# A ternary feed-forward on four engines: a butterfly on GpSimd before the token rotation, three small tasks moved to ScalarE and GpSimd

## The chip, the cores and the metric

The kernel runs on one core of one Trainium2 chip. The metric is the device time of one execution in microseconds (us), the median of several runs. The engines are named as in the profile: PE is TensorE, PEld its weight loads, DVE VectorE, ACT ScalarE, POOL GpSimd, SP SyncE.

## What is computed

The reference is a network of four layers on x, four batches of 512 tokens with 512 dimensions, in float32. Each layer adds its result to x: an attention over a context (layer A), a feed-forward with ternary weights (layer B), a self-attention with 32 heads (layer C) and a routed mixture of 8 experts (layer D). The change touches layer B only:

```python
def h_bitlinear(x, w):
    xq = act_quant(fwht(x))      # 8-bit absmax quantisation per token
    wq = weight_quant(w)         # ternary, scale is mean(|w|)
    return jnp.einsum('bsh,oh->bso', xq, wq)
gate = h_bitlinear(hidden_states, w_gate)
up = h_bitlinear(hidden_states, w_up)
return h_bitlinear(jax.nn.silu(gate) * up, w_down)
```

`fwht` is the normalised Walsh-Hadamard transform along the last axis, 512 wide for the tokens and 2048 wide for the product of gate and up. The input of the layer is the normalised x (mean and deviation of each token). A Hadamard matrix of size 2n is made of four blocks H, H, H and minus H of size n, so the first half of the transform of 512 values is the 256-wide transform of the sum of their halves, and the second half that of their difference.

## The kernel before

Every engine has its own queue, in which the order of the work is written out by hand; semaphores join the queues. Layer B is done batch by batch (`phase_b(b)` on each engine, b from 0 to 3), and within a batch in tiles of 128 tokens (`st` from 0 to 3). While batch b is in its second half, the tokens of batch b+1 are made ready. The order in one batch, with the names of the functions:

- POOL: `half_rotated(b, r)` for seven of eight pairs of chunks (L848), three of the second parts of the inner rotation, `second_part_of(b, 1..3)` for their first half of 1024 columns (L853), then `normed_batch(b+2)`: after the deviation (L801) four instructions of 128x512, which subtract the mean and multiply by the reciprocal deviation (L864). `normed_batch(1)` stands at the end of layer A's part.
- PE: eight rounds of `gate_and_up` (L2580), with the transposes of the normalised tokens of batch b+1, `tokens_transposed` (L2529), within the last ones; then `tokens_rotated(b+1, st)` (L2541). This multiplies by the 512x512 Hadamard matrix, kept as four blocks of 128 rows, in two parts of the tokens each (a first part in rounded float32 and a second part, which is what the rounding left), so 8 matmuls of 512 columns for a tile. Then `inner_rotated(b, st, g)` (L2595), 8 matmuls for each of four groups g of 512 columns; between them `tokens_quantised_transposed(b+1)` (L2550), `inner_quantised_transposed(b, st)` (L2607), `down_projected(b, st)` (L2625) and `scales_spread(b+1)` (L2561). The last tiles' down projections fall between the rounds of the next batch.
- DVE: gates and their products (L1892, L1906), the last `half_rotated` (L1913), the second stage of the inner rotation (`second_stage`, L1920 and L1921, 128x1024 each), the second parts (`second_part_of`, L1926; for tile 0 both halves, for the other tiles the second half), the token scales (`token_scales`: L1834 to L1854), `inner_scales` (L1933 to L1940), quantisation (L1873, L1947); after `quantised_inner(b, 0)` it does `scale_diagonals(b+1)` (L1867, four instructions of 128x128, and L1869) and `quantised_tokens_t(b+1)` (L1885, two copies of 128x1024 bf16 from PSUM to SBUF).
- ACT: `first_part` (L1309, two of 128x1024 for a tile; the first half's semaphore releases POOL, the second's DVE), `rotated_rows` (L1316, PSUM to SBUF), `scaled_tokens` (L1287), `scaled_inner` (L1323), `inner_transposed` (L1331, one of 128x2048 bf16).

`inner_rotated(b, st, g)` waits at g = 0 for the first half's second part and at g = 2 for the second half's; `down_projected(b, 0)` waits for ACT's `inner_transposed(b, 0)`, and, because it writes the bank from which the quantised tokens are copied, for `quantised_tokens_t(b+1)`. `scales_spread` waits for the diagonals. In the fourth batch there is no next batch; in its place POOL and ACT work on the first chunks of layer C (`dims_split`, L993 and L994; `chunk_out`, L1404), and PE transposes them.

## Time and profile before

| what | us |
|---|---|
| median of 3 runs | 1669.87 |
| lowest and highest run | 1669.15, 1671.94 |
| span of the profiled execution | 1670.3 |
| layer B in the trace, roughly | 130 to 490 |
| layer C (attention), roughly | 490 to 925 |
| layer D (experts), to the end | from 925 |

The profiled execution is given by its span alone; no other time of it is recorded. Times in the trace count from the start of the span. The profile gives for each instruction when it began and how long it took; an instruction that waits inside, for a port for example, shows a longer time. The idle time of an engine stands before the instruction that ended it, with the instruction on another engine that released it. Matmuls are pipelined, so the distance of their starts, not their duration, is what one costs. Batches 1 and 2 of layer B repeat each other with a period of 89.0 us, and batch 0 ends in the same way.

### The profile page before, as it was taken

How to read it: one execution, taken by the hardware profiler on the slowest of the kernel's cores; microseconds unless marked ns; L12 is line 12 of the kernel's file. 1: busy time of each engine (PE TensorE's matmuls, PEld its weight loads, DVE VectorE, ACT ScalarE, POOL GpSimd, SP SyncE). 2: the span in 40 equal slices, each digit the busy share in tenths (PEclk: the TensorE clock that was granted, in tenths of full speed). 3: DMA queues.
4: the chain of work that ended last, by engine and by line, in shares of the span. 5: the costliest groups of instructions: out<-in, count | busy, mean ns of one | idle time of the engine just before them, and what ended most of it. 6: DMA issues, size and time to landing. Idle time of an engine off the chain costs nothing.

```text
span 1670.3 us, 24439 instructions
## 1 busy us (share of the span) xinstructions
PE 1567.2 (94%) x8124; PEld 1047.5 (63%) x8150; DVE 948.0 (57%) x1539; ACT 717.6 (43%) x1160; POOL 702.1 (42%) x479
## 2 busy tenths in 40 slices
PE   6869999999889999999899899999999999999998
PEld 4555657565543434434333778788788888788886
DVE  6998979796878897887885622222122222222221
ACT  5885646455547777777677211111111111111111
POOL 1124251633513125254354765670862180930064
PEclk9889999999898999999999999999999999999999
DMA  9189800000231445243430625231440140530088
GB/s 357 56 305 386 291 1 1 0 1 1 84 94 47 123 132 149 82 126 111 148 114 28 224 70 189 82 120 32 182 176 26 59 155 26 188 127 26 26 140 213
DMA packets 90944, 196.16 MB, mean 117 GB/s; under 512 B 7153, under 2 KB 9074, under 8 KB 90226
## 3 DMA queue, kind: packets, MB, share of 16 engines
q1 hardware_dynamic: 71746, 156.68, 28.2%
q0 software_dynamic: 7168, 17.04, 4.5%
q10 hardware_dynamic: 11952, 21.43, 3.9%
q8 instruction: 45, 0.74, 0.2%
q14 instruction: 33, 0.27, 0.1%
HBM read 113.28 MB, written 81.32 MB: 117 GB/s over the span
## 4 chain that ended last, share of the span: by engine, by line
PE 68%; DVE 16%; POOL 6%; ACT 4%; issue 3%; DMA 3%; another core or an unknown queue 0%; SPq 0%; POOLq 0%; DVEq 0%; ACTq 0%
PE psum L2929 11%; PE psum L2931 11%; PE psum L2930 11%; PE psum L2580 6%; DVE neg_max L2057 5%; PE psum L2782 5%; PE psum L2771 5%; PE psum L2744 4%; POOL expert_weight_parts L1052 3%; PE psum L2625 3%; PE psum L2595 2%; DMA w_of_even_expert<-in_L_ffn_w 2%; PE psum L2953 2%; POOL expert_weight_parts L1051 1%; DVE inner_rotated_t_second L1926 1%
## 5 line engine op out<-in xcount | busy, mean ns | idle before, releaser
L2057 DVE TENSOR_REDUCE neg_max<-psum 128x2 f32<-128x1024 f32 x248 | 291.3, 1220 | 49.5 <-PE psum L2744 48.3
L1420 ACT ACTIVATE probabilities<-psum 128x512 f32<-128x512 f32 x512 | 271.7, 601 | 85.2 <-PE psum L2771 81.3
L2199 DVE TENSOR_TENSOR expert_inner<-psum,expert_inner 128x512 f32<-128x512 f32 x78 | 53.9, 692 | 388.7 <-ACT expert_inner L1526 378.6
L2929 PE MATMUL psum<-expert_weight_parts,sorted_tokens_t_first 128*128 x624 | 250.8, 402 | 8.8 <-POOL expert_weight_parts L1052 5.1
L2930 PE MATMUL psum<-expert_weight_parts,sorted_tokens_t_first 128*128 x624 | 246.8, 396 | 0.0
L2931 PE MATMUL psum<-expert_weight_parts,sorted_tokens_t_second 128*128 x624 | 246.8, 395 | 0.0
L1526 ACT ACTIVATE expert_inner<-psum 128x512 f32<-128x512 f32 x78 | 46.7, 599 | 396.7 <-PE psum L2931 396.7
L2771 PE MATMUL psum<-query_rows,key_rows 50*128 50x512 f32 x512 | 179.3, 444 | 4.1 <-ACT probabilities L1420 3.0
L2744 PE MATMUL psum<-key_rows,query_rows 48*128 48x512 f32 x496 | 170.6, 491 | 11.7 <-DVE neg_max L2057 5.8
L2929 PEld LDWEIGHTS psum<-expert_weight_parts,sorted_tokens_t_first 128*128 128x128 f32 x624 | 117.7, 189 | 37.4 <-issue 11.1
L2782 PE MATMUL psum<-probabilities,value_and_one 128*32 128x512 f32 x1024 | 140.3, 620 | 0.8 <-ACT probabilities L1420 0.7
L2931 PEld LDWEIGHTS psum<-expert_weight_parts,sorted_tokens_t_second 128*128 128x128 f32 x624 | 117.8, 189 | 27.4
L2930 PEld LDWEIGHTS psum<-expert_weight_parts,sorted_tokens_t_first 128*128 128x128 f32 x624 | 117.9, 189 | 26.1
L2771 PEld LDWEIGHTS psum<-query_rows,key_rows 50*128 50x128 f32 x512 | 80.1, 190 | 85.2 <-ACT probabilities L1420 39.3
L1051 POOL CAST expert_weight_parts<-wo_of_expert 128x2048 fp32r<-128x2048 f32 x16 | 30.3, 1897 | 241.5 <-PE psum L2931 241.5
L1531 ACT ACTIVATE expert_inner_t_first<-psum 128x512 fp32r<-128x512 f32 x78 | 42.5, 596 | 201.8 <-PE psum L2953 201.8
L2929 PE MATMUL psum<-expert_weight_parts,expert_inner_t_first 128*128 128x512 f32 x312 | 125.8, 403 | 1.6 <-DVE expert_inner_t_second L2209 1.6
L2931 PE MATMUL psum<-expert_weight_parts,expert_inner_t_second 128*128 128x512 f32 x312 | 122.3, 392 | 0.0
L2930 PE MATMUL psum<-expert_weight_parts,expert_inner_t_first 128*128 128x512 f32 x312 | 121.9, 391 | 0.0
L2226 DVE TENSOR_SCALAR expert_out<-psum,row_weight 128x512 f32<-128x512 f32 x39 | 29.3, 751 | 160.8 <-PE psum L2931 156.8
L1010 POOL TENSOR_TENSOR x_tiles<-x_tiles,attended_normed 128x256 f32<-128x256 f32 x31 | 22.7, 733 | 211.2 <-DVE attended_normed L2104 211.2
L2595 PE MATMUL psum<-hadamard,inner_rotated_t_first 128*128 128x512 f32 x256 | 104.5, 408 | 7.0 <-DVE inner_rotated_t_second L1926 7.0
(316 smaller groups left out, 2924.3 us busy)
## 6 DMA issues: line engine op xcount, KB each, us to landing
sorted_x<-zero_rows SPq DMA_DIRECT2D x9, 3960.0 KB, 30.5
w_of_odd_expert<-in_L_ffn_w SPq DMA_DIRECT2D x8, 2048.0 KB
wo_of_expert<-in_L_ffn_wo SPq DMA_DIRECT2D x7, 2048.0 KB, 8.6
query_rows<-query_rows_of_units SPq DMA_DIRECT2D x64, 192.0 KB, 3.5
w_of_even_expert<-in_L_ffn_w SPq DMA_DIRECT2D x6, 2048.0 KB, 11.6
sorted_tokens<-sorted_x ACTq DMA_DIRECT2D x39, 264.0 KB, 2.8
sorted_y<-expert_out ACTq DMA_DIRECT2D x39, 256.0 KB
query_rows_of_units<-dims_first SPq DMA_DIRECT2D x32, 256.0 KB
```

What stands on the lines that cost most here:

```text
L1052: last = nc.gpsimd.tensor_tensor(w_r[:, at + BLOCK + s:at + BLOCK + s + BLOCK // 2], w, first_part, ALU.subtract)
L1420: nc.scalar.activation(prob[t % 2][:, i * SEQ:(i + 1) * SEQ], bank[4 + n % 3], ACT.Exp, scale=HD ** -0.5).then_inc(c_e, 1)
L2057: nc.vector.tensor_reduce(of_pair[:, p, st, :], ring(("max", (m, i))).rearrange("p (h n) -> p h n", h=2), AX.X, ALU.max, negate=True).then ...
L2199: nc.vector.tensor_tensor(h, bank[2 * half + 1], h, ALU.mult).then_inc(e_h, 1)
L2580: last = nc.tensor.matmul(bank[4 + 2 * w + h], wgu_t[w][:, k * FF + f * P:k * FF + (f + 1) * P], q_t[:, k * SEQ:(k + 1) * SEQ], start=(k = ...
L2595: last = nc.tensor.matmul(bank[4 + g], y[:, at:at + P], had[:, k * D:(k + 1) * D], start=(k + part == 0), stop=(k + part == DC))
L2744: done = nc.tensor.matmul(ring(job)[:, h * SEQ:(h + 1) * SEQ], q_r[m % 4][rows, p * SEQ + st * P:p * SEQ + (st + 1) * P], k_r[m % 4][rows, ...
L2771: nc.tensor.matmul(bank[4 + n % 3], k_r[u % 4][rows, t * P:(t + 1) * P], q_r[u % 4][rows, p * SEQ:(p + 1) * SEQ], start=True, stop=True).t ...
L2782: last = nc.tensor.matmul(bank[7][32 * h:32 * h + 32, :], v_u[u % KVH][:, t * 32:(t + 1) * 32], prob[t % 2][:, h * SEQ:(h + 1) * SEQ], sta ...
L2929: nc.tensor.matmul(out_bank, hi[:, cols], w_r[:, bass.ds(w_at, 512)], start=start, stop=False)
L2930: nc.tensor.matmul(out_bank, hi[:, cols], w_r[:, bass.ds(w_at + BLOCK, 512)], start=False, stop=False)
L2931: return nc.tensor.matmul(out_bank, lo[:, cols], w_r[:, bass.ds(w_at, 512)], start=False, stop=stop)
```

## The change

The four edits in words:

1. `normed_batch` on POOL makes, for each tile, the sum and the difference of the two halves of x (two instructions of 128x256), then normalises each half in place (the sum with twice the mean, the difference without a mean): 16 instructions and a small one for twice the mean, where there were four. `tokens_rotated(b, st)` for b of 1 to 3 multiplies with 256 columns of the first two blocks of the Hadamard matrix: 8 matmuls of 256 columns for a tile.
2. The second part of tile 0's second half goes from DVE to POOL, where it stands before the other second parts.
3. The scale diagonals of batches 1 to 3 go from DVE to ACT, after `inner_transposed(b, 0)`.
4. The two copies of the transposed quantised tokens of batches 1 to 3 go from DVE to ACT, after `first_part(b, 3)` and before `rotated_rows(b, 2, 0)`.

The diff, cut to its core (batch 0's tokens keep the old way):

```diff
def second_part(b, st, h):
 
-            if st and h == 0:
-                return b_zlo, (ST - 1) * b + st
-            return b_zlo0, (ST + 1) * b + st + h + 1
+            if h != (st == 0):
+                return b_zlo0, ST * b + st + 1
+            return b_zlo, ST * b + st + 1
...
             def second_part_of(b, st):
-                pool.wait_ge(b_zhi, 2 * (b * ST + st) + 1)
-                half = HALVES[0]
+                h = int(st == 0)
+                pool.wait_ge(b_zhi, 2 * (b * ST + st) + h + 1)
+                half = HALVES[h]
...
+                c.inc(nc.gpsimd.tensor_tensor(twice_mean[:], mv[:, 0:2 * ST:2], mv[:, 0:2 * ST:2], ALU.add))
+                halves = [[h_n[:, st * D + h * D // 2:st * D + (h + 1) * D // 2] for h in range(2)] for st in range(ST)]
                 for st in range(ST):
-                    nc.gpsimd.tensor_scalar(h_n[:, st * D:(st + 1) * D], tiles(X, b * ST + st), mv[:, 2 * st:2 * st + 1],
-                                            rstd[:, st:st + 1], ALU.subtract, ALU.mult).then_inc(b_normed, 1)
+                    x = [X[:, (b * ST + st) * D + h * D // 2:(b * ST + st) * D + (h + 1) * D // 2] for h in range(2)]
+                    c.inc(nc.gpsimd.tensor_tensor(halves[st][0], x[0], x[1], ALU.add))
+                    c.inc(nc.gpsimd.tensor_tensor(halves[st][1], x[0], x[1], ALU.subtract))
+                c.wait()
+                for st in range(ST):
+                    c.inc(nc.gpsimd.tensor_scalar(halves[st][0], halves[st][0], twice_mean[:, st:st + 1],
+                                                  rstd[:, st:st + 1], ALU.subtract, ALU.mult))
+                    nc.gpsimd.tensor_scalar(halves[st][1], halves[st][1], rstd[:, st:st + 1], None, ALU.mult).then_inc(b_normed, 1)
...
+                second_part_of(b, 0)
                 for st in range(1, ST):
                     second_part_of(b, st)
...
             def scaled_token(b, st):
-                act.wait_ge(b_fac, b + 1)
+                act.wait_ge(b_fac, 2 * b + 1)
...
+            def scale_diagonals(b):
+                act.wait_ge(b_fac, 2 * (b + 1))
+                for st in range(ST):
+                    last = nc.scalar.activation(diag[:, st * P:(st + 1) * P], ident[:], ACT.Copy, scale=tok_scale[:, st:st + 1])
+                last.then_inc(b_dg, 1)
+
+            def quantised_tokens_t(b):
+                for half in range(2):
+                    act.wait_ge(b_qt, b * ST + 2 * half + 2)
+                    nc.scalar.activation(q_t[:].rearrange("p (k t n) -> p t k n", k=DC, t=ST)[:, 2 * half:2 * half + 2],
+                                         bank_b[2 + half].rearrange("p (t k n) -> p t k n", t=2, k=DC), ACT.Copy).then_inc(b_qts, 1)
...
                 first_part(b, 3)
+                if more:
+                    quantised_tokens_t(b + 1)
                 rotated_rows(b, 2, 0)
...
                 inner_transposed(b, 0)
+                if more:
+                    scale_diagonals(b + 1)
                 scaled_inner(b, 1)
...
             def token_scale_columns(b):
                 for st in range(ST):
                     s = slice(st, st + 1)
-                    c.inc(nc.vector.tensor_scalar(tok_scale[:, s], am_c[:, s], 1.0 / 127.0, None, ALU.mult))
+                    last = nc.vector.tensor_scalar(tok_scale[:, s], am_c[:, s], 1.0 / 127.0, None, ALU.mult)
+                last.then_inc(b_fac, 1)
...
-            def scale_diagonals(b):
-                c.wait()
-                if b == 0:
-                    dve.wait_ge(a_sim, BATCH * ST)
+            def first_scale_diagonals():
+                dve.wait_ge(b_fac, 2)
+                dve.wait_ge(a_sim, BATCH * ST)
                 for st in range(ST):
                     last = nc.vector.tensor_scalar(diag[:, st * P:(st + 1) * P], ident[:], tok_scale[:, st:st + 1], None, ALU.mult)
                 last.then_inc(b_dg, 1)
+
+            def inner_scale_made(b):
+                dve.wait_ge(b_fac, 2 * (b + 1))
                 c.inc(nc.vector.tensor_scalar(inner_scale[b % 2][:], tok_scale[:], w_mean[:, 1:2], HAD_FF, ALU.mult, ALU.mult))
...
                 second_part_of(b, 0, 0)
-                second_part_of(b, 0, 1)
                 second_stage(b, 1)
...
                 if more:
-                    scale_diagonals(b + 1)
-                    quantised_tokens_t(b + 1)
+                    inner_scale_made(b + 1)
                 second_part_of(b, 3, 1)
...
                     for part, h in enumerate((first_part_at(b)[:, st * D + k * P:st * D + (k + 1) * P], h_lo(b, st)[:, k * P:(k + 1) * P])):
-                        last = nc.tensor.matmul(bank[st], h, had[:, k * D:(k + 1) * D], start=(k + part == 0), stop=(k + part == DC))
+                        if b == 0:
+                            last = nc.tensor.matmul(bank[st], h, had[:, k * D:(k + 1) * D], start=(k + part == 0), stop=(k + part == DC))
+                        else:
+                            half, j = k // 2, k % 2
+                            last = nc.tensor.matmul(bank[st][:, half * D // 2:(half + 1) * D // 2], h, had[:, j * D:j * D + D // 2],
+                                                    start=(j + part == 0), stop=(j + part == 2))
```

## Rows read from the trace of the kernel before

**Rows 1.** The page's first part: busy time of each engine over the span.
```profile
PE 1567.2 (94%) x8124; PEld 1047.5 (63%) x8150; DVE 948.0 (57%) x1539; ACT 717.6 (43%) x1160; POOL 702.1 (42%) x479
```

**Rows 2.** Busy time by stretches of one batch; columns as in the header.
```profile
core 0: us, PE busy (x) PEld busy (x) DVE busy (x) ACT busy (x) POOL busy (x), PEclk, DMA share, GB/s
...
249.20:338.20 89.00, 85.79 (x452) 55.25 (x457) 76.59 (x138) 48.03 (x57) 36.04 (x22) 1.00 0.00 1
...
427.20:516.20 89.00, 72.64 (x353) 44.63 (x355) 73.81 (x91) 44.18 (x54) 25.42 (x35) 0.85 0.30 83
```

**Rows 3.** Waits of PE within 249.2 to 338.2 us: total, times, longest us.
```profile
PE psum L2550 <- DVE uantised_tokens_of_batch L1873: 1.5, 1, 1.5
PE psum L2625 <- DVE quantised_t L1885: 1.0, 1, 1.0
PE psum L2625 <- ACT inner_quantised_t L1331: 0.3, 1, 0.3
```

**Rows 4.** Chain that ended last, at 282.7 us: start us, us, what.
```profile
282.73 3.40 PE psum L2625 x15
```

**Rows 5.** DVE timeline, 249 to 258 us: start, us, engine, line, op, tiles, idle.
```profile
252.05 0.69 DVE L1829 TENSOR_TENSOR ormed_tiles_t_second<-psum,normed_tiles_t_first 128x512 fp32r<-128x512 f32 x1 [0.23 <-ACT normed_tiles_t_first L1283]
...
256.13 2.36 DVE L1926 TENSOR_TENSOR inner_rotated_t_second<-inner_t,inner_rotated_t_first 128x1024 fp32r<-128x1024 f32 x2 [0.53 <-ACT inner_rotated_t_first L1309]
```

**Rows 6.** DVE timeline, 269 to 284 us.
```profile
271.10 2.27 DVE L1926 TENSOR_TENSOR inner_rotated_t_second<-inner_t,inner_rotated_t_first 128x1024 fp32r<-128x1024 f32 x1
...
276.90 1.21 DVE L1947 TENSOR_SCALAR quantised_tokens<-normed_or_scaled_tokens 128x2048 bf16<-128x2048 f32 x1
278.04 3.00 DVE L1867 TENSOR_SCALAR token_scale_diagonals<-ident,token_scale 128x128 f32<-128x128 f32 x4
...
281.09 1.27 DVE L1885 COPY quantised_t<-psum 128x1024 bf16<-128x1024 bf16 x2
```

**Rows 7.** POOL timeline, 255 to 296 us.
```profile
269.88 2.40 POOL L853 TENSOR_TENSOR inner_rotated_t_second<-inner_t,inner_rotated_t_first 128x1024 fp32r<-128x1024 f32 x1 [5.55 <-ACT inner_rotated_t_first L1309]
278.15 2.41 POOL L853 TENSOR_TENSOR inner_rotated_t_second<-inner_t,inner_rotated_t_first 128x1024 fp32r<-128x1024 f32 x1 [5.86 <-ACT inner_rotated_t_first L1309]
```

**Rows 8.** ACT timeline, 264 to 300 us.
```profile
277.01 2.01 ACT L1309 ACTIVATE inner_rotated_t_first<-inner_t 128x1024 fp32r<-128x1024 f32 x2 [2.25 <-DVE inner_t L1921]
278.93 1.07 ACT L1316 ACTIVATE inner_rotated_rows<-psum 128x512 f32<-128x512 f32 x2
279.88 1.88 ACT L1331 ACTIVATE inner_quantised_t<-psum 128x2048 bf16<-128x2048 bf16 x1
```

**Rows 9.** ACT groups by line and form: xcount, busy us, mean ns, idle.
```profile
L1165 ACT ACTIVATE down_ternary_t<-psum 128x1024 bf16<-128x1024 bf16 x6 | 6.0, 1004 | 0.0
...
L1113 ACT ACTIVATE kv_gram<-psum 128x128 f32<-128x128 f32 x4 | 1.1, 269 | 1.9 <-PE psum L2346 1.9
```

**Rows 10.** POOL groups by line and form, same columns.
```profile
L864 POOL TENSOR_SCALAR normed_tokens_of_batch<-x_tiles,ln_mean_var,ln_rstd 128x512 f32<-128x512 f32 x12 | 28.2, 2358 | 0.3
...
L1010 POOL TENSOR_TENSOR x_tiles<-x_tiles,attended_normed 128x256 f32<-128x256 f32 x31 | 22.7, 733 | 211.2 <-DVE attended_normed L2104 211.2
```

**Rows 11.** PE timeline, 247 to 258 us.
```profile
249.17 0.39 PE L2541 MATMUL psum<-hadamard,ormed_tiles_t_second 128*128 128x512 f32 x1
...
250.56 0.39 PE L2541 MATMUL psum<-hadamard,ormed_tiles_t_second 128*128 128x512 f32 x1
250.79 1.03 PE L2529 MATMUL psum<-ident,normed_tokens_of_batch 128*128 128x128 f32 x8
```

**Rows 12.** PE timeline, 428 to 436 us, fourth batch.
```profile
434.97 0.76 PE L2595 MATMUL psum<-hadamard,inner_rotated_t_first 128*128 128x512 f32 x1 [7.04 <-DVE inner_rotated_t_second L1926]
435.53 0.63 PE L2595 MATMUL psum<-hadamard,inner_rotated_t_second 128*128 128x512 f32 x1
```

**Rows 13.** Busy time in the attention stage, columns as rows 2.
```profile
624.80:628.20 3.40, 2.37 (x17) 1.02 (x17) 3.01 (x5) 2.10 (x4) 3.40 (x3) 1.00 0.04 8
628.20:631.60 3.40, 3.40 (x18) 1.78 (x10) 2.23 (x5) 1.27 (x4) 3.40 (x3) 0.50 0.36 92
```

More of the change, by code:

```diff
@@ L112, in network @@
         rstd = keep.tile("ln_rstd", [P, ST])
+        twice_mean = keep.tile("ln_twice_mean", [P, ST])
         half_neg = keep.tile("minus_half", [P, ST])
@@ L1812, in phase_a @@
                 token_scale_columns(0)
-                scale_diagonals(0)
+                first_scale_diagonals()
+                inner_scale_made(0)
                 sum_reciprocals(3)
@@ L1823, in phase_a @@
                 weight_out(17)
-                quantised_tokens_t(0)
+                first_quantised_tokens_t()
                 weight_out(19)
@@ L1878, in quantised_tokens, with first_quantised_tokens_t @@
                     quantised_token(b, st)
-            def quantised_tokens_t(b):
-                if b == 0:
-                    dve.wait_ge(a_done, BATCH * ST)
+            def first_quantised_tokens_t():
+                dve.wait_ge(a_done, BATCH * ST)
                 for half in range(2):
-                    dve.wait_ge(b_qt, b * ST + 2 * half + 2)
+                    dve.wait_ge(b_qt, 2 * half + 2)
                     nc.vector.tensor_copy(q_t[:].rearrange("p (k t n) -> p t k n", k=DC, t=ST)[:, 2 * half:2 * half + 2],
```

## The prediction

> **What bounds the kernel now.** I read the page's busy times first: PE is busy for 94% of the span [rows 1], but that is an average over four layers. The busy time by batch is the second view. In batch 1 of layer B PE is busy for 85.79 of 89.00 us and DVE for 76.59, ACT for 48.03 and POOL for 36.04, all at full clock (1.00); in the fourth batch the clock's mean is 0.85 [rows 2]. So PE has 3.2 us of idle time in a batch, and only this, or work that PE drops while nobody else is late, can be won. The third view says who ends that idle time: DVE's quantised tokens 1.5 us, DVE's copy `quantised_t` before the down projection 1.0, ACT's `inner_quantised_t` 0.3, DVE's second part of the tokens 0.2 [rows 3]. In the chain of waits the down projection of tile 0 starts at 282.73 [rows 4]. The question for every edit is thus which wait ends last at 250 to 258 us, at 273 and at 282.7; the same times plus 89.0 hold for batch 2, less 89.0 for batch 0.
>
> **The butterfly on PE.** Matmuls of 512 columns start 0.232 us apart (seven starts from 249.17 to 250.56) [rows 11], so a tile costs 1.86 us and the 12 tiles of batches 1 to 3 cost 22 us. No row has 256 columns of this type. The nearest rows bound one: below, half of 0.232; above, the same 0.232, if the weight load sets the pace. The eight transposes of 128 columns begin at 250.79 and the next matmul at 251.58 [rows 11], about 0.10 each, so a weight load fits into 0.12, and I take half: 0.93 us off a tile, 3.7 off a batch, 11.1 in all. The Trainium skill (TensorE: Matmul & The Clock Gate, "Back-to-back issue gap") gives 262 cycles for 256 columns and 518 for 512; by it 0.85 us would leave each tile.
>
> This is what the tile costs, not what the time gains. The next work on PE, `inner_rotated(1, 0, 0)`, needs DVE's second part, which begins at 256.13 after 0.53 us of waiting for ACT [rows 5] and takes 1.2; PE's last rotation matmul starts at about 257.4. Both arrive together: PE's work is hidden under the DVE chain from the last gates through half rotation, second stage and ACT's first part. Only one link of that chain waits for PE: DVE waited 0.23 us at 252.05 for ACT's first part of the tokens [rows 5]. So the halving brings 0.2 to 0.3 us a batch at this point, and PE is idle for the other 3.4 us in several pieces. The ends for the sum are 0 and 11.1 us; I take 0, since the next meeting point (273.3, below) doesn't move.
>
> **The second part to POOL.** DVE loses half of 2.36 us [rows 5], 1.18. POOL takes 2.40 for one [rows 7]. The two engines don't run such work side by side: DVE's L1926 at 271.10 took 2.27 us instead of 1.18 while POOL's ran from 269.88 to 272.28; 272.28 and 1.1 is its end, 273.37 [rows 6, 7]. The four diagonals at 278.04 took 3.00 us beside POOL's at 278.15 for the same reason. The new POOL instruction becomes ready at about 256.9, just when DVE goes on with the second stage of tile 1, two instructions with both inputs in SBUF. So DVE waits for 2.40 and saves 1.18 and 0.3: its token scales come 0.9 us later, not 1.2 earlier. This is covered: 0.9 us later, DVE would come to L1926 at 272.0, and POOL holds it until 272.28 in any case [rows 6, 7]. I take 0; with that cover gone it costs 0.9 a batch. The rule against this edit is in the Trainium skill (GPSIMD Engine Reference, "Engine selection" and "Key points"): elementwise work on two tensors belongs on VectorE, and GpSimd shares its SBUF interfaces with VectorE. The trace agrees, 2.40 against 1.18.
>
> **Diagonals and copies to ACT.** DVE loses 3.05 us (278.04 to 281.09) less 0.2 for the inner scale, and 1.2 for the copies [rows 6]. Its next instruction, L1926 of tile 3, meets POOL's, which ends at 280.56 [rows 7], and so ends near 281.7, not 283.4. That relieves `inner_scales(1)`, for which PE doesn't wait [rows 3].
> ACT gets the work on the path. After `first_part` (277.01, 2.01 us) it now goes on at 278.93 with the rows and at 279.88 with `inner_quantised_t`, 1.88 [rows 8]. The new copies stand before these. A copy of 1024 bf16 columns from PSUM costs 1.00 on ACT [rows 9], two cost 1.9 with their overlap of 0.1. So `inner_quantised_t` starts at 281.8, ends at 283.7, and PE begins 0.25 later, at 283.9 instead of 282.73 [rows 4]: 1.2 us late. The ends for the copies: below, DVE's 0.64 each [rows 6], which gives 0.5 us a batch; above, the 2.01 of `first_part` for two, 1.3. From there PE is never idle for long [rows 3], so all of it stays: three batches, **+3.6 us**. The queue behind the copies: `rotated_rows(2, 0)`, whose bank PE wants only after the down projection, and `scaled_inner(1)`, which is earlier anyway. The four diagonals cost at most 0.27 each [rows 9], 1.1 us, done by 284.8; `scales_spread` comes after the down projection: 0.
>
> **POOL's normalisation.** Before: four of 2.08 (mean with collisions 2.36) [rows 9, 10], 8.3 to 9.4 us. After: eight of 0.733 [rows 10] are 5.9, four two-step ones of 1.04 (half of 2.08) and four one-step ones of 0.5 to 1.04, in all 12 to 14.5. The 3 to 6 us more lie in POOL's 53 idle us a batch [rows 2]; the tokens are wanted a phase later. If that cover were gone, PE's inner rotation would be late by as much. In layer A, where `normed_batch(1)` meets a busy DVE, collisions added 0.28 a piece; I add 0.4 us in all, ends 0 and 3. Here the first tile's semaphore comes 8 us later, without anyone at the door.
>
> **Fourth batch.** No copies; DVE has 1.18 less and POOL 2.40 more, while PE stands 7.04 us [rows 12] for a chain that ends before the moved instruction. 0, ends -1 and +2.
>
> **The clock.** After those 7.04 us PE's matmuls took 0.63 instead of 0.39 [rows 11, 12]: the lower level, 1.2 GHz. In the attention a stretch with PE busy for 2.37 of 3.40 us is followed by one at 0.50 [rows 13]. After the change PE has 3.4 us more idle time at 251 to 257, and its wait before the down projection grows from 1.0 to 2.2 us. These are six places in three batches. A fall as short as that of rows 13 costs at most half of 3.4 us, 1.7. Ends 0 and six times 1.7, 10.2; I take one fall, **+1.7**, since the present waits of 1.5 and 1.0 us caused none [rows 2].
>
> **Sum.** 3.6 + 0.4 + 1.7 = +5.7 us on the span of 1670.3, 1676.0. The span stands 0.4 us above the median of the runs, 1669.87, so I give 1675.6.
>
> **Rivals.**
> - The relief reaches PE (faster, 0.23). For it: DVE ends 2.5 of PE's 3.2 idle us [rows 3], and DVE loses 5.2 us of work a batch. Against: ACT's order and POOL's hold. If ACT's copies slip in before `first_part(3)` is released or end by 281.5, both waits go: 3 x 2.5 = 7.5 us, 1662.4. With only the first wait gone, 1665.5. The halved matmuls could add to it only where DVE isn't late.
> - No difference (0.25). ACT's copies cost nearer 0.64, or a third of the delay is won back, and the clock stays up: 0 to 3.3 us, 1670 to 1673.
> - POOL's second half is late (slower, 0.07). If DVE keeps the port through both second-stage instructions, POOL ends at 261.7, PE wants it at 260.8: 0.9 x 3 more, 1678.3.
> - The clock falls at all six places (slower, 0.08): 10.2 in place of 1.7, 1684.
> - The forecast has 0.37, its own range is 1673.3 to 1679.
>
> A measurement of this kernel can tell about 0.2%, 3.3 us, from no change. My range is 1664 to 1681.5: it takes in the second faster case and a second or third fall of the clock. Faster 0.23, within 0.2% 0.25, slower 0.52.
>
> **What the new profile would show.** L2541 with 256 columns, starts 0.12 apart, and PE idle behind them at 252 to 257; DVE's second stage of tile 1 at 2.3 or more for one of its instructions beside a POOL L853 line; the wait of L2625 ended by ACT's `inner_quantised_t`, 2.2 us long in each of three batches; the period between batches 90.2 us instead of 89.0. I am wrong if that wait is no longer than 1.0, if the period is below 89, or if the attention or expert layer changes its length.

## The result and the profile after

| | before | after |
|---|---|---|
| median of 5 runs, us | 1669.66 | 1679.99 |
| lowest and highest run | 1669.15, 1671.94 | 1677.35, 1684.53 |
| span of the profiled execution | 1670.3 | 1678.2 |
| its mean granted clock | 0.975 | 0.971 |

The kernel is slower: ratio 1.0061, 95% interval 1.0045 to 1.0077. That is 10.3 us where 5.7 were forecast. In another comparison of the same two kernels (e2 below) it was 1.0078, 1.0058 to 1.0098, 13.7 us. The two profiled spans are only 7.9 us apart. Where both are recorded, a span is 1.8 to 1.9 us below its run's time, so the span of 1670.3 probably belongs to the slowest of the runs before, 1671.94.

The page's busy times and its line of the clock, kernel after:

```profile
PE 1566.9 (93%) x8149; PEld 1043.6 (62%) x8150; DVE 946.5 (56%) x1517; ACT 727.4 (43%) x1178; POOL 734.1 (44%) x522
...
PEclk9889998999997999999999999999999999999999
```

PE is as busy as before, 1566.9 against 1567.2 us [rows 1], although 96 of its matmuls are half as wide. Busy time that doesn't fall where work was halved suggests that other matmuls ran slower. The next view has the granted clock to go with it: busy times and granted clock of the kernel after, for the stretches from the end of `gate_and_up` in one batch to that of the next (three rows), then for layers B and C.

```profile
core 0: us, PE busy (x) PEld busy (x) DVE busy (x) ACT busy (x) POOL busy (x), PEclk, DMA share, GB/s
159.70:251.10 91.40, 85.05 (x459) 54.53 (x457) 75.31 (x131) 51.49 (x64) 44.28 (x36) 0.98 0.43 157
251.10:344.60 93.50, 87.75 (x459) 56.05 (x457) 75.30 (x131) 51.26 (x64) 44.40 (x36) 0.95 0.00 1
344.60:434.90 90.30, 83.93 (x450) 53.55 (x449) 72.11 (x120) 50.19 (x62) 37.90 (x23) 0.98 0.00 1
128.50:500.10 371.60, 342.87 (x1820) 217.57 (x1820) 302.76 (x478) 205.29 (x247) 172.33 (x125) 0.96 0.26 90
500.10:922.90 422.80, 399.25 (x2378) 163.31 (x2376) 347.60 (x460) 306.49 (x576) 166.21 (x219) 0.96 0.37 106
```

The same stretches were 89.0, 89.0 and 88.1 us before (the third has the fourth batch's work in it), all at a clock of 1.00. They are now 91.4, 93.5 and 90.3, together 9.1 us more, at 0.98, 0.95 and 0.98. Layer B took 361.7 us before and takes 371.6; layer C went from 424.4 to 422.8, layer D, the rest of the span, from 754.3 to 755.3. In these two profiled executions the loss is all in layer B (the part ahead of it is 1.4 us shorter). The pair on one chip, e1 and e2, will say otherwise.

**Who ends PE's waits.** The waits of PE from 160 to 430 us, kernel after:

```profile
PE psum L2573 <- DVE ormed_tiles_t_second L1857: 6.8, 6, 1.7
PE psum L2658 <- ACT inner_quantised_t L1354: 5.9, 3, 2.0
PE psum L2583 <- DVE uantised_tokens_of_batch L1904: 4.4, 3, 1.5
```

Three rows, three things (a fourth of 1.3 us is left out). The rotation of the tokens (L2573) waits 6.8 us for DVE's rounding remainder L1857. The down projection (L2658) waits 5.9 us for ACT, 2.0 each time, where it waited 1.0 for DVE's copy and 0.3 for ACT [rows 3]. The wait for the quantised tokens, which one would expect to shrink with less work on DVE, is as it was, 1.5 us in a batch.

**The rotation and the clock.** PE's timeline of batch 1, kernel after:

```profile
251.36 0.28 PE L2573 MATMUL psum<-hadamard,ormed_tiles_t_second 128*128 128x256 f32 x1
251.48 0.28 PE L2573 MATMUL psum<-hadamard,normed_tiles_t_first 128*128 128x256 f32 x1
...
254.78 0.39 PE L2573 MATMUL psum<-hadamard,normed_tiles_t_first 128*128 128x256 f32 x1 [0.60 <-DVE ormed_tiles_t_second L1857]
...
257.65 0.58 PE L2573 MATMUL psum<-hadamard,normed_tiles_t_first 128*128 128x256 f32 x1 [1.65 <-DVE ormed_tiles_t_second L1857]
258.03 0.41 PE L2573 MATMUL psum<-hadamard,ormed_tiles_t_second 128*128 128x256 f32 x1
258.24 0.41 PE L2573 MATMUL psum<-hadamard,normed_tiles_t_first 128*128 128x256 f32 x1
...
260.05 0.63 PE L2628 MATMUL psum<-hadamard,inner_rotated_t_second 128*128 128x512 f32 x1
```

A matmul of 256 columns starts 0.12 us after the last one, and a tile costs 0.94 us. But PE then stands, 0.60 us before tile 2 and 1.65 before tile 3, since these are made ready by DVE behind other work. From 258.03 the same matmuls start 0.21 apart, and the inner rotation's 512 columns take 0.63 us instead of 0.39 [rows 12]. The view by stretches says that this is the clock. Two falls of batch 1, each behind the stretch before it:

```profile
253.60:257.00 3.40, 1.80 (x13) 1.39 (x12) 3.40 (x5) 0.32 (x1) 0.00 (x0) 1.00 0.00 0
257.10:263.90 6.80, 6.25 (x19) 5.26 (x20) 6.28 (x5) 2.56 (x4) 2.46 (x1) 0.50 0.00 0
284.40:287.70 3.30, 1.34 (x7) 0.78 (x6) 3.30 (x3) 3.30 (x5) 0.12 (x1) 1.00 0.00 0
287.80:291.20 3.40, 3.40 (x9) 1.21 (x8) 1.10 (x7) 3.22 (x6) 0.00 (x0) 0.51 0.01 2
```

Read the columns PE and PEclk in pairs. PE was busy for 1.80 of 3.40 us and for 1.34 of 3.30 at full clock, and behind each the clock was 0.50, the first time for 6.8 us, the second for 3.4. The first is the rotation, the second the wait before the down projection. The rotation brought two more falls of 3.4 us, at 168.3 in the batch before and at 352.6 in the one behind. Before, the three batches had none; in layer B the clock was low only in its first microseconds and behind the fourth batch's wait of 7 us.

**ACT ahead of the down projection.** ACT's timeline in batch 1, kernel after:

```profile
281.00 2.01 ACT L1332 ACTIVATE inner_rotated_t_first<-inner_t 128x1024 fp32r<-128x1024 f32 x2 [2.82 <-DVE inner_t L1951]
282.91 1.92 ACT L1314 ACTIVATE quantised_t<-psum 128x1024 bf16<-128x1024 bf16 x2
...
285.67 1.90 ACT L1354 ACTIVATE inner_quantised_t<-psum 128x2048 bf16<-128x2048 bf16 x1
287.43 1.29 ACT L1308 ACTIVATE token_scale_diagonals<-ident,token_scale 128x128 f32<-128x128 f32 x4
```

and PE's:

```profile
287.62 2.22 PE L2658 MATMUL psum<-down_ternary_t,inner_quantised_t 128*128 128x512 bf16 x5 [1.96 <-ACT inner_quantised_t L1354]
```

L1314 is the pair of new copies, 1.92 us. They stand between `first_part` and the rows, L1354 begins behind them, and PE begins when it ends. The four diagonals L1308 come after it and hold up nobody.

**POOL and DVE.** The second part of tile 0, on POOL and then on DVE beside it, kernel after:

```profile
259.11 2.46 POOL L855 TENSOR_TENSOR inner_rotated_t_second<-inner_t,inner_rotated_t_first 128x1024 fp32r<-128x1024 f32 x1 [8.03 <-ACT inner_rotated_t_first L1332]
...
302.41 2.05 POOL L873 TENSOR_SCALAR normed_tokens_of_batch<-normed_tokens_of_batch,ln_twice_mean,ln_rstd 128x256 f32<-128x256 f32 x1 [0.21 <-POOL normed_tokens_of_batch L870]
304.45 0.93 POOL L875 TENSOR_SCALAR normed_tokens_of_batch<-normed_tokens_of_batch,ln_rstd 128x256 f32<-128x256 f32 x1
305.37 1.23 POOL L873 TENSOR_SCALAR normed_tokens_of_batch<-normed_tokens_of_batch,ln_twice_mean,ln_rstd 128x256 f32<-128x256 f32 x1
...
312.06 2.50 POOL L849 TENSOR_TENSOR inner_half_rotated_t<-inner_t 128x512 f32<-128x512 f32 x2 [0.30 <-DVE inner_t L1936]
```

```profile
259.26 3.39 DVE L1950 TENSOR_TENSOR inner_t<-inner_half_rotated_t 128x1024 f32<-128x1024 f32 x1
262.58 1.21 DVE L1951 TENSOR_TENSOR inner_t<-inner_half_rotated_t 128x1024 f32<-128x1024 f32 x1
```

DVE's L1950 takes 3.39 us beside POOL's 259.11, its twin L1951 takes 1.21 alone. In POOL's own rows the normalisation follows: in place, a step with two operations takes 1.23 us (2.05 beside DVE) and one with a single operation 0.93. With the eight sums and differences ahead of it, from 296.46 on, the whole ends at 311.76, 15.3 us, and POOL's next work waits only for DVE (0.30).

### The profile page after: what moved, and what is told of

Read it like the earlier page. It is cut to its first block and busy times, and to the rows that moved or that the text cites. A ratio compares the mean times of both kernels' runs of the same rounds, so it can differ in the third digit from the quotient of the medians.

```text
span 1678.2 us, 24506 instructions
## 1 busy us (share of the span) xinstructions
PE 1566.9 (93%) x8149; PEld 1043.6 (62%) x8150; DVE 946.5 (56%) x1517; ACT 727.4 (43%) x1178; POOL 734.1 (44%) x522
## 6 DMA issues: line engine op xcount, KB each, us to landing
w_of_even_expert<-in_L_ffn_w SPq DMA_DIRECT2D x6, 2048.0 KB, 11.7
```

## The experiments

Twelve kernels ran, each against the kernel before on the same chip. Four of them are the change with one part undone or covered, five have one or two parts alone or moved, one warms the fourth batch, and two repeat the kernels before and after. Besides the time, each run recorded its mean granted clock, and this turned out to be the second number to read. Within the runs of one kernel the time goes with it: 29 runs of the kernel before on one chip had clocks from 0.974 to 0.982, and a fitted line loses 1.1 us for each 0.001 (on the two other chips 1.2 and 0.9). So each difference is split below into the part that goes with the clock, at 1.1 us for 0.001, and the rest. The split is a correlation, not a cause, and not exact: with the copies late the rest is 4.9 to 8.0 us, more than the 3.3 to 3.6 that their batches show at full clock. Layer B's length is from the one profiled execution, against 361.7 and 362.3 us in two of the kernel before.

| kernel | ratio, 95% interval | difference us | mean clock, before's | by the clock, rest | layer B |
|---|---|---|---|---|---|
| e2, all parts | 1.0078, 1.0058 to 1.0098 | +13.7 | 0.9727, 0.9793 | 7.3, 6.4 | 370.4 |
| a1, copies back | 1.0042, 1.0026 to 1.0059 | +7.3 | 0.9725, 0.9797 | 7.9, -0.6 | 363.3 |
| a2, no butterfly | 1.0058, 1.0038 to 1.0078 | +11.7 | 0.9751, 0.9797 | 5.1, 6.6 | 371.8 |
| a3, second part back | 1.0081, 1.0060 to 1.0102 | +13.9 | 0.9740, 0.9797 | 6.3, 7.6 | 367.9 |
| a4, all parts, PE kept busy | 1.0086, 1.0064 to 1.0107 | +15.7 | 0.9727, 0.9797 | 7.7, 8.0 | 367.5 |
| b1, butterfly alone | 1.0062, 1.0048 to 1.0076 | +10.0 | 0.9720, 0.9796 | 8.4, 1.6 | 365.8 |
| b2, late copies alone | 1.0057, 1.0044 to 1.0071 | +8.3 | 0.9765, 0.9796 | 3.4, 4.9 | 368.6 |
| b3, early copies alone | 1.0011, 1.0002 to 1.0021 | +1.2 | 0.9766, 0.9796 | 3.3, -2.1 | 359.4 |
| b4, second part alone | 1.0021, 1.0009 to 1.0033 | +3.8 | 0.9768, 0.9793 | 2.8, 1.0 | 363.2 |
| c2, early copies and more | 1.0011, 0.9999 to 1.0024 | +1.1 | 0.9786, 0.9796 | 1.1, 0 | 362.4 |
| d1, b3 and a warm fourth batch | 1.0000, 0.9987 to 1.0012 | +0.7 | 0.9790, 0.9793 | 0.3, 0.4 | 359.4 |
| e1, the kernel before | 1.0001, 0.9988 to 1.0014 | +0.1 | 0.9790, 0.9793 | 0.3, -0.2 | 362.3 |

### One part undone: a1 to a4

**a1, the copies back on DVE.**

```diff
                 first_part(b, 3)
-                if more:
-                    quantised_tokens_t(b + 1)          # ACT
...
                     inner_scale_made(b + 1)
+                    dve_quantised_tokens_t(b + 1)      # DVE, as before
```

> The changed kernel (1680.0 us, before 1669.7) with the two copies of the transposed quantised tokens done by DVE again, right after the inner scale; the diagonals stay on ACT. Theory (ACT's copies end last before the first down projection, 1.2 us a batch, and the longer stand lets PE's clock fall): PE's wait before that down projection falls from 2.0 us to about 0.5 and its clock stays up at 288 us; three times 1.9 us and one or two falls of 1.7, so 1670.9 to 1674.3. Rival (the falls of the clock in the rotation are the whole loss): no more than 1 us gained, 1679 to 1680. Rival (the collision of POOL and DVE at the second stage is the loss): 1680.

The wait of the down projection for ACT is gone, and layer B is 7 to 8 us shorter than in the two profiles of the whole change. The rest beside the clock's part is near zero. So the late copies are most of what costs in layer B, and the 7.3 us that are left go with the clock. Most of them aren't in layer B, by the profiles: it is 1.0 us longer than in e1, which ran on another chip, and layer C is 5.9 us longer (421.3 for 415.4).

The batch of a1 without a fall, by stretches:

```profile
251.60:339.80 88.20, 83.62 (x459) 53.23 (x457) 74.86 (x133) 49.57 (x61) 44.27 (x36) 1.00 0.00 1
```

It is 0.8 us shorter than the 89.0 before and 1.9 shorter than the 90.1 of the whole change at full clock. So the other three parts together gain 0.8 us there, and the late copies take 1.9. Before the down projection PE waits for nobody in a1. In b1 and b4 below, which leave the diagonals on DVE, the wait of 1.0 us for DVE's copies is still there. With the diagonals off DVE the copies come right behind the inner scale, at 280.85 in a1. No run has the diagonals alone.

**a2, the old normalisation and rotation**, all else as after.

```diff
-                c.inc(nc.gpsimd.tensor_tensor(twice_mean[:], ...))
...
+                    nc.gpsimd.tensor_scalar(h_n[:, st * D:(st + 1) * D], tiles(X, b * ST + st), mv[...], rstd[...], ALU.subtract, ALU.mult)
...
-                        if b == 0:
+                        # every batch: 512 columns, had[:, k * D:(k + 1) * D]
```

> The changed kernel without the butterfly: POOL normalises 128x512 as before, PE rotates with 512 columns; the other three edits stay. Theory (the butterfly brings nothing on the path and lets the clock fall in front of the inner rotation, with 1 to 1.7 us each and 6.8 us long in one batch): granted clock 1.00 over 150 to 280 us, 2.5 to 5 us faster than the changed kernel, 1675 to 1677.5. Rival (the butterfly is worth its 11 us of PE work, or a part, and the rest costs more): slower than 1680, up to 1690. Rival (it does nothing): 1680.

The clock of 1.00 that was expected up to 280 us didn't come. The falls in the rotation are gone and layer B is no shorter, 371.8: all three batches now have a fall in the wait before the down projection. Undoing one cause of falls didn't remove them, it moved them. The first batch, kernel a2:

```profile
160.50:252.60 92.10, 88.42 (x458) 55.52 (x457) 74.49 (x131) 51.42 (x63) 37.77 (x23) 0.98 0.43 155
```

The first batch of a4, below, has the butterfly and its one fall in the same place, and takes 91.8. So where the clock is the same, the butterfly is worth about 0.3 us a batch (a4's added matmuls lie in waits).

**a3, the second part of tile 0 back on DVE.**

```diff
-                second_part_of(b, 0)                   # POOL
...
                 second_part_of(b, 0, 0)
+                second_part_of(b, 0, 1)                # DVE
```

> The changed kernel with the second part of tile 0's second half on DVE again. Theory (POOL's 2.4 us delay DVE's token scales by 0.9 us net, but DVE would wait for POOL at the next second part anyway): within 1.5 us of the changed kernel, 1678.5 to 1680.5, DVE's second stage of tile 1 at 1.21 again in place of 3.39. Rival (the collision is on the path, 0.9 to 1.2 us a batch): 1676.4 to 1677.3.

No gain that the whole time shows. Its profile has two falls, both in the rotation, and a batch without a fall takes 89.7 us, 0.4 below the 90.1 of the whole change.

**a4, PE kept busy in the rotation.** Ahead of the waits of tiles 2 and 3, 8 and 16 matmuls of 256 columns into the tile's own bank, which the tile then overwrites.

```diff
+                if b and st >= 2:
+                    for n in range(8 * (st - 1)):
+                        nc.tensor.matmul(bank[st][:, 0:D // 2], first_part_at(b)[...], had[:, 0:D // 2], start=True, stop=True)
                 pe.wait_ge(b_lo, b * ST + st + 1)
```

> The changed kernel with PE kept busy in the rotation of the tokens: 24 matmuls of 256 columns a batch, whose result nobody reads, stand before tiles 2 and 3 of the token rotation, where PE otherwise waits for DVE. They add 2.9 us of PE work a batch and no other work. Theory (idle PE lets the clock fall): no stretch at 0.50 at the start of the inner rotation, time as without the butterfly, 1675 to 1677.5. Rival (the loss of the butterfly comes from POOL's longer normalisation or elsewhere, not from the clock): 1680, or 1 to 9 us slower if the added work isn't hidden.

The view by stretches of a4, its three batches:

```profile
161.70:253.50 91.80, 87.76 (x483) 56.52 (x481) 74.14 (x131) 51.43 (x64) 44.37 (x36) 0.98 0.42 154
253.50:343.60 90.10, 86.11 (x483) 56.06 (x481) 74.13 (x131) 51.53 (x64) 44.28 (x37) 1.00 0.00 1
343.60:432.90 89.30, 85.31 (x474) 55.27 (x473) 71.08 (x120) 50.25 (x62) 37.91 (x24) 1.00 0.00 1
```

The rotation causes no fall any more; the one in the first batch is in the wait before the down projection. Two batches are at 1.00, and they show what the change costs with the clock up: 90.1 us against 89.0, 89.3 against 88.1. That is the forecast's 1.2, within 0.1. But the whole kernel is none the faster for it, where 2.5 to 5 us were expected, and its mean clock is as low as e2's. Its profile has the time and the low clock elsewhere. Against e1, again on another chip, layer B is 5.2 us longer, layer C 6.4 (421.8 for 415.4) and layer D 3.3 (759.7 for 756.4). The clock was low for 34.1 us within layer C where e1 has 20.5, and for 19.7 us in layer D where e1 has 13.1.

### One part alone: b1, b2, b4

**b1, the butterfly alone**, copies, diagonals and second part on DVE as before: a1's and a3's edits, and

```diff
                 inner_transposed(b, 0)
-                if more:
-                    scale_diagonals(b + 1)             # ACT
...
                 if more:
+                    dve_scale_diagonals(b + 1)
                     inner_scale_made(b + 1)
```

> The kernel before with the butterfly alone (POOL's sums and differences, rotation with 256 columns); everything else as before. Batch periods of the kernel before are 89.0, 89.0 and 88.1 us. Theory (the halved matmuls lie behind DVE's chain, their only effect is idle PE and at times a fall of the clock): a batch without a fall keeps its period within 0.4 us, a batch with a fall at the start of the inner rotation is 1.2 to 1.7 us longer; in all 0 to 5 us slower than before. Rival (PE's dropped work of 3.7 us a batch comes through once nothing else is changed): 3 to 11 us faster.

Each batch has one fall, in the rotation. Layer B is 4 us longer, as expected, but the whole kernel 10.0, twice the 5 that were expected at most, and 8.4 of these go with the clock. Halving this work of PE made the kernel slower, more outside layer B than in it. One of PE's waits in layer C of b1:

```profile
PE psum L2803 <- DMA query_rows<-neg_max_second_rows: 4.1, 2, 3.8
```

One wait of 3.8 us for a transfer; the longest for this one in e1 is 0.7. It is met again under e2.

**b2, the late copies on ACT alone.** Edits 1, 2 and 3 undone as in a2, a3 and b1; of the change only this stands:

```diff
                 first_part(b, 3)
+                if more:
+                    quantised_tokens_t(b + 1)
```

> The kernel before with the two copies of the quantised tokens on ACT alone, after its first part of tile 3, as in the change. Theory: PE's wait before the first down projection is 2.0 us and ended by ACT's inner_quantised_t in each of three batches; the period is 90.2 without a fall of the clock and 91.9 with one in the down projection, so 3.6 to 8.7 us slower than before. Rival (the copies are harmless, the loss of the change is the butterfly's and POOL's): within 1 us of before.

Its three batches:

```profile
160.90:252.70 91.80, 87.44 (x452) 55.65 (x457) 75.62 (x136) 50.25 (x59) 36.04 (x22) 0.98 0.43 155
252.70:344.50 91.80, 87.44 (x452) 55.58 (x457) 75.60 (x136) 50.26 (x59) 36.03 (x22) 0.98 0.00 1
344.50:433.80 89.30, 85.00 (x445) 54.37 (x449) 72.50 (x125) 49.07 (x57) 35.76 (x22) 1.00 0.00 1
```

and PE's wait for `inner_quantised_t`:

```profile
PE psum L2644 <- ACT inner_quantised_t L1344: 7.5, 6, 2.2
```

The first down projection waits 2.2 us, 1.2 more than before, and the third batch, at 1.00, is 89.3 against 88.1: the delay arrives whole. The first two batches have a fall in that wait and are 2.8 longer than 89.0, so a fall of 3.4 us costs another 1.6 us there. The 8.3 us of the whole are within the 3.6 to 8.7 that were expected.

**b4, the second part on POOL alone.** Copies, diagonals and butterfly as before; of the change only this stands:

```diff
+                second_part_of(b, 0)                   # POOL
...
                 second_part_of(b, 0, 0)
-                second_part_of(b, 0, 1)                # DVE
```

> The kernel before with the one edit that moves the second part of tile 0's second half to POOL. Theory (DVE's 0.9 us delay is covered by its wait for POOL at the next second part): batch periods 89.0 within 0.3 us, time within 1 us of before. Rival (the collision is on the path): periods 89.9 to 90.2, 2.7 to 3.6 us slower.

PE's waits, kernel b4:

```profile
PE psum L2570 <- DVE uantised_tokens_of_batch L1893: 2.9, 3, 1.0
PE psum L2615 <- POOL inner_rotated_t_second L855: 1.4, 3, 0.5
```

The inner rotation (L2615) waits 0.5 us in each batch for POOL, and the wait for the quantised tokens (L2570) is 1.0 instead of 1.5, so that PE's waits sum to 8.9 us where they are 9.0 in e1. Batches are 89.3, 89.2 and 88.4 us long all the same, 0.2 to 0.3 more; where this is, the waits don't show. The periods are within what was expected, the 3.8 us of the whole kernel are not (1 us was). 2.8 of them go with the clock.

### Could it have been a gain: b3, c2, d1

**b3, the copies on ACT, before `first_part(b, 3)` instead of behind it**, and nothing else of the change.

```diff
+                if more:
+                    quantised_tokens_t(b + 1)
                 first_part(b, 3)
-                if more:
-                    quantised_tokens_t(b + 1)
```

> As b2_only_copies, but the two copies stand in ACT's queue before its first part of tile 3, in the 2.2 us in which ACT waits for DVE's second stage (from 274.8 to 277.0 in the trace of before). Theory (only the place of the copies in ACT's queue made them cost): the wait before the first down projection shrinks below the 1.0 us of before, 0.7 to 1.0 us a batch are won, 2 to 3 us faster than before. Rival (ACT's copies cost more wherever they stand, or DVE's relief meets POOL's hold of the port): within 1 us of before or slower.

ACT's timeline and PE's waits, kernel b3:

```profile
274.01 1.95 ACT L1304 ACTIVATE quantised_t<-psum 128x1024 bf16<-128x1024 bf16 x2
276.37 2.01 ACT L1322 ACTIVATE inner_rotated_t_first<-inner_t 128x1024 fp32r<-128x1024 f32 x2 [0.40 <-DVE inner_t L1940]
```

```profile
PE psum L2569 <- DVE uantised_tokens_of_batch L1893: 4.4, 3, 1.5
PE psum L2644 <- ACT inner_quantised_t L1344: 2.0, 6, 0.4
```

The copies run at 274.01, in time in which ACT otherwise waits: `first_part` still waits 0.40 us for DVE behind them. The six waits of the down projections sum to 2.0 us, where they are 4.0 in e1. The batches are 88.3, 88.3 and 87.4 us, 0.7 shorter than before, all at 1.00. So the first rival of the prediction was a matter of one call's place in ACT's order. The whole time doesn't show it: +1.2 us, interval just above 1, where 2 to 3 us faster was expected. The rest beside the clock's part is -2.1, which is what three batches of 0.7 give, and the part that goes with the clock, 3.3, is larger. In its profile layer B is 2.9 us shorter than in e1, and layer C 2.4 longer (417.8).

**c2, b3 with the diagonals on ACT too and DVE's quantisation of the tokens before `inner_scales(b, 0)`.**

```diff
                 second_stage(b, 2)
+                if more:
+                    quantised_tokens(b + 1)
                 inner_scales(b, 0)
...
                 second_part_of(b, 2, 1)
-                if more:
-                    quantised_tokens(b + 1)
```

> As b3_copies_early, with the scale diagonals on ACT as in the change, and with DVE's quantisation of the next batch's tokens moved before inner_scales(b, 0), out from behind the second part that waits for POOL. Theory (the 1.5 us wait of PE for the quantised tokens is made by DVE's order): that wait goes, 1.2 to 2.0 us a batch won over b3_copies_early's 0.7 to 1.0, in all 5 to 8 us faster than before. Rival (the inner scales come 1.3 us later and delay PE's next transposes by as much): no faster than b3_copies_early.

PE's wait for the quantised tokens is gone (4.4 us in b3), but ACT gets its work later and `inner_quantised_t` becomes the wait, 2.7 us before the first down projection. The batches are 89.2, 89.1 and 88.2 us: a wait taken away at one place came back, longer, at the next. The 5 to 8 us that were expected didn't come.

**d1, b3 with 28 matmuls of 512 columns into a free bank in the fourth batch,** where PE stands for 7 us; nothing reads them.

```diff
                     for chunk in (CTX_CHUNK, 0, 1, 2):
                         chunk_transposed(0, chunk)
+                    pe.wait_ge(c_xs, 2)
+                    for n in range(28):
+                        nc.tensor.matmul(bank[0], had[:, 0:P], had[:, 0:D], start=True, stop=True)
```

> As b3_copies_early, with 28 matmuls whose result nobody reads in PE's 7.0 us of waiting before the inner rotation of the fourth batch. Theory (idle PE lets the clock fall): granted clock 1.00 over 425 to 445 us in place of 0.50, inner rotation of the fourth batch at 0.23 us a matmul from its first one, layer B 1.5 to 2.5 us shorter than b3_copies_early's 359.4, so 3.8 to 4.8 us below the kernel before in layer B. Rival (the fall doesn't come from the idle time): the clock is at 0.50 there as before, no gain.

Stretches in the fourth batch of b3 (its fall) and of d1:

```profile
430.80:437.60 6.80, 4.62 (x11) 3.69 (x12) 5.60 (x6) 2.55 (x4) 0.81 (x1) 0.51 0.52 186
424.00:489.20 65.20, 54.28 (x289) 38.09 (x291) 52.59 (x64) 36.19 (x39) 23.43 (x16) 0.95 0.37 104
```

```profile
424.20:488.40 64.20, 58.73 (x318) 41.87 (x320) 51.99 (x64) 36.48 (x39) 24.00 (x16) 1.00 0.38 106
```

The clock stays at 1.00 through the fourth batch, and the batch is only 1 us shorter, 64.2 us for 65.2. Layer B as a whole is no shorter than b3's, 359.4 in both, where 1.5 to 2.5 us were expected. So the fall does come from the idle time, and it cost little here. PE's waits for ACT's `inner_quantised_t` in the batch grew from 3.7 to 4.8 us with the clock up, which fits a chain through DVE and ACT that sets the end. The kernel is level with before, 1.0000.

### The kernels again: e1, e2

e1 is the kernel before and e2 the kernel after, both unchanged.

> The kernel before, unchanged, on the chip of this group, with a profile: what layer B, the attention and the expert layer take here, and how far two sets of runs of one kernel differ. Ratio 1.000 within 0.1%; layer B's batch periods 89.0, 89.0, 88.1 as in the first trace; what differs lies in the attention, where stretches at granted clock 0.50 come and go.

> The changed kernel, unchanged, on the same chip: 8 to 13 us above the kernel before, of it 7 to 10 us in layer B, whose periods are 90.1 without a fall of the clock and 1.2 to 1.7 more with each fall. If the rest of the difference is in the attention, its stretches at clock 0.50 last longer there than in the kernel before by about twice that difference.

Two profiles of one kernel differ. Stretches of e2, three batches:

```profile
160.60:251.80 91.20, 84.18 (x451) 54.48 (x456) 75.27 (x131) 51.48 (x64) 44.17 (x36) 0.98 0.43 155
251.80:341.90 90.10, 83.06 (x452) 53.30 (x456) 74.17 (x131) 51.56 (x64) 44.30 (x37) 1.00 0.00 1
341.90:435.40 93.50, 86.52 (x445) 55.02 (x449) 72.29 (x120) 50.13 (x62) 37.86 (x24) 0.95 0.00 1
```

In e2 the middle batch has no fall and takes 90.1 us; in the profile after it had two. So the batches that fall are not the same in two runs of one program. Layer C was 424.4 us in the first profile of before and 415.4 in e1, 422.8 and 421.0 in the two of after. PE's wait in e2:

```profile
739.03 0.79 PE L2804 MATMUL psum<-query_rows,key_rows 50*128 50x512 f32 x1 [3.41 <-DMA query_rows<-neg_max_second_rows]
```

From this wait on the clock was low for 10.2 us. It is the wait for the second of two rows of 8 KB, written behind the transfers of `query_rows` and `key_rows`. The kernels with the butterfly have it: the longest is 4.2 us in a1, 4.9 in a3, 3.3 in a4, 3.8 in b1 and 3.4 in e2, and only the first profile of after is without it. In the eight profiles without the butterfly it is 1.1 us at most. Layer C goes the same way: 420.5 to 421.8 us in those five, 413.7 to 419.6 in the profiles without the butterfly on the same chips (a2 419.3, b2 413.7, b3 417.8, b4 415.0, c2 413.7, d1 419.6, e1 415.4). The gap in layer C is narrow for a2 and d1, so the wait is the clearer sign. Why the transfer is late wasn't tried. That layer C starts later isn't the reason: layer B ends at 501.0 us in a2 and 498.6 in b2, which lack the wait, and at 494.2 and 496.0 in a1 and b1, which have it.

The profiles of e1 and e2 can be set side by side, as they are of one chip. e2 is 13.8 us longer, 8.1 in layer B, 5.6 in layer C and 0.1 in the rest. Its clock was low for 97.6 us in all, for 77.8 in e1. Of the 19.8 more, 10.2 are in layer B (13.6 in the three batches, less 3.4 in the fourth, whose fall is shorter), 6.8 in layer C behind the late rows and 2.8 in layer D. The expectation had low stretches in layer C longer by twice what the layer loses; they are longer by 1.2 times that, and the late rows themselves make PE wait 2.7 us more.

## Why the prediction was right, and where it was not

The direction, the range (1664 to 1681.5 holds 1679.99) and the main mechanism held; the size was short by 4.6 us. That the range held is in part luck: by e2's ratio, 1.0078, the same change would have given 1682.9. And what layer C lost in e2, 5.6 us, stands in none of the sum's terms.

- **The copies on ACT, +1.2 a batch: right.** The waits of L2625, now L2658, were 1.3 us a batch before (1.0 and 0.3) and 2.5 at full clock in e2 and b2, with 2.2 the longest; a batch at full clock grew by 1.1 (a4, e2) and 1.2 (a4, b2). The price of 1.9 for two was 1.92. The lower end given for them, 0.5, should be 0.6 by its own terms (1.9 less twice 0.64, from 1.2).
- **The butterfly, 0 on the path: nearly right.** The matmuls start 0.12 apart, as taken. The Trainium skill (TensorE: Matmul & The Clock Gate, "Back-to-back issue gap") gives 262 cycles for 256 columns, as an estimate 0.11 us at 2.4 GHz, a little under the trace's 0.12. PE idles behind them, as said, and 0.3 us a batch come through (a2 against a4), the 0.2 to 0.3 that the prediction worked out and then left out. What the idle time does to the clock was handed to the clock term, and what the butterfly does to layer C has no term.
- **The clock, +1.7 for one fall: the step that failed.** The argument was that waits of 1.5 and 1.0 us had caused none [rows 2]. It looked at each wait by itself. The rotation now has waits of 0.60 and 1.65 us and short matmuls around them, and PE was busy for 1.80 of the 3.40 us ahead of a fall. The profiles show four falls ahead of the fourth batch in the kernel after and three in e2, one of 6.8 us in each, in place of one of 3.4. A batch with one fall of 3.4 us is 1.1 to 1.7 us longer than one without: after 91.4 and 90.3 against 90.1 and 89.2, b2 91.8 against 90.2 (its third batch's 89.3 and the 0.9 by which that batch was shorter before), a3 91.4 against 89.7, a4 91.8 against 90.1. That bears out 1.7 as the upper end for each; the number of falls was the error. The rival "at all six places", at 0.08 and 1684, is as far from the median as the forecast, and nearer in what happened: five times 3.4 us at 0.50 in the profile after.
- **Layer B in sum.** Three batches at 1.1 are 3.3, and what is left above that in each, 1.3, 3.4 and 1.1, is put down to its falls: 9.1 us in all. Forecast were 5.3. The 1.1 is itself a sum, 1.9 for the late copies less the 0.8 that the other parts gain (a1).
- **The second part, 0: 0.2 to 0.4 a batch** (b4, and a3's batch from the other side). DVE's L1950 took 2.2 us more beside POOL (3.39 against 1.21) where 2.40 was forecast. The Trainium skill (GPSIMD Engine Reference, "Key points") has GpSimd share its SBUF interfaces with VectorE, with contention when a VectorE instruction has two inputs in SBUF; the trace agrees, as L1950 has two. The third rival, POOL's half being late for PE, priced 0.9, is real: PE waited 0.5 for it in every batch of b4, a2 and a4 and once in a1 and e2; in b4 a wait for the quantised tokens shorter by as much followed.
- **The diagonals, 0: right for their cost** (1.29 us on ACT, behind L1354). Their relief of DVE was put at nothing for PE, which holds with the late copies; with the copies left on DVE it took away the wait before the down projection (a1).
- **The normalisation, 12 to 14.5 us: 15.3**, since a single operation took 0.93 where 0.5 to 1.04 was taken and two took 1.23 and not 1.04. Hidden as said: POOL's next work waited for DVE. The 0.4 for layer A's part: the first batch's `gate_and_up` ended at 159.7 in both profiles, so 0.
- **The fourth batch, 0: right**, 65.2 us from `gate_and_up` to the end of layer B against 65.8, with a fall of 6.8 us for one of 10.2.
- **"I am wrong if the attention changes its length."** One profile each can't answer it, as layer C of the kernel before itself differs by 9 us between two, on two chips. But on the later chips layer C is 420.5 to 421.8 us in five profiles with the butterfly and 413.7 to 419.6 in seven without, and a1 and b1 lost 7.3 and 10.0 us with only 1.6 and 4 of them in layer B. So by this sign the prediction was wrong: a part of the loss, 5.6 of 13.8 us in e1 and e2, is in the attention, in kernels that do no more work there. The late rows go with it, and how the butterfly makes them late is open.
- **The first rival (faster) was right about the place.** b3 shows the slot on ACT that it named, worth 0.7 a batch where it had 2.5, and b3 isn't faster than before as a whole.

## What to carry to other kernels

Before halving the work of an engine that waits for another one right behind it, ask what the idle time does: on PE it bought 0.3 us of 3.7 a batch, and it came with a fall of the clock in most batches. When a step moves to another engine, its place in that engine's order decides the sign: one call earlier the same copies ran inside a wait, one call later they delayed the bound engine by all of 1.2 us. And read the mean granted clock of every run beside its time, and the length of every layer, since a part may cost little in the layer that it touches and still lose elsewhere.

## What was not expected of the hardware

- Falls of the clock are not a fixed property of a kernel: the same batch of the same program had falls of 6.8 and 3.4 us in one profile and none in another (93.5 and 90.1 us).
- Twenty-nine runs of one program spread over 0.974 to 0.982 in mean clock and follow it in time at about 1.1 us for 0.001.
- At full clock through the fourth batch, d1 gained 1 us where the fall had halved PE's speed for 6.8.
- On GpSimd a tensor with scalars of 128x256 in place took 0.93 us with one operation and 1.23 with two, more than half of the 2.08 that 128x512 with two took from another buffer.
